# First layer's stored values: from SyncE's transfers at the end of the edge count to ScalarE's queue in attention's fifth unit

## The chip, the cores and the metric

The kernel runs on one core of a Trainium2 chip. The metric is device time of one execution in microseconds (us). Engines are named as in the profile: PE (TensorE, with PEld for its weight loads), DVE (VectorE), ACT (ScalarE), POOL (GpSimd) and SP (SyncE, which here only issues transfers).

## The reference

A graph of 1250 nodes with 512 features and 20000 edges. After a layer norm come two layers of graph attention with 8 heads, each followed by a feed-forward net and batch norms; then a small gated MLP on decoded nibbles.

```python
for l in range(L):                       # 2 layers
    q = ((x @ Wq[l].T + bq[l]) * scaling).reshape(n, H, DH)
    k = (x @ Wk[l].T).reshape(n, H, DH)
    v = (x @ Wv[l].T).reshape(n, H, DH)
    scores = jnp.einsum('ehd,ehd->eh', q[tgt], k[srcidx])
    p = jnp.exp(scores - m[tgt])         # softmax over each target's edges
    agg = segment_sum(w[:, :, None] * v[srcidx], tgt)
    x = _batchnorm(x + agg.reshape(n, D) @ Wo[l].T + bo[l], ...)
    x = _batchnorm(x + relu(x @ W1[l].T + b1[l]) @ W2[l].T + b2[l], ...)
```

## The kernel before

Attention is computed densely: how often an edge joins each pair of nodes is counted into a 1250 by 1250 matrix, whose logarithm (or a very negative number where there is no edge) is added to the scores as a bias. The program is a row of blocks. At the end of a block every engine waits until all engines have come to its end; a transfer need only be issued by then, not landed.

**First block (edge count and first layer's projections).** For each of ten tiles of 125 targets PE counts edges, ACT takes logarithms, DVE combines, and SP stores the tile to `edge_bias` in DRAM (`bias_out`, L536). In the gaps, and after the last tile, PE runs the projections in the order of `JOBS`: q, then v, then k. ACT copies v out of PSUM twice: the first four heads into `v_pair`, where attention will use them, and all of it into `v_stage` (both in `projected`). The keys are split into a high part (`k_stack`, ACT, L344) and a low part (`k_lo`, DVE, L376). The low part of each chunk c of 128 features is copied by SP to the other 64 partitions of `k_stack` (`k_stacked`, L401, two transfers of 64 partitions by 1250 numbers). The block's SP program ends with `stacked` for the first two passes' queries (L461), `k_stacked` for chunks 0 and 1, `values_out`, and `k_stacked` for chunks 2 and 3. `values_out` (L406) stores `v_stage`, 1250 by 512 numbers, to the DRAM tensor `values` in two transfers, of 120 and of 5 partitions (2400 and 100 KB). PE ends the block with 12 idle matmuls (`keep_clock`, L103).

**Attention block of each layer.** A pass n is one pair of heads by one group of two target tiles; 20 passes of 4 units make 80 units u. The program of each engine is written in slots. In slot s, PE computes the three score pieces of unit s (L945) and transposes the probabilities of unit s-3 (L959), and in two of four slots it multiplies a finished pass by the values (L974). DVE adds the bias and finds the peaks (L1041, L1064), copies the middle transposed piece (L1032) and forms the inverse of the mass (L1048, L1050). ACT in slot s copies the first transposed piece of unit s-3 (L1000), takes the exponential of unit s-1 (L1011), and copies the third piece of unit s-3 (L1000). POOL divides (L925) and splits the queries (L449, L451). A pass's output is copied to `attn` by ACT (`out_of`, L1007), first in slot 10. `attn` lies in the same SBUF region as `v_stage`, so the first `out_of` waits until `values` is stored. SP loads the rest of the bias in four parts (`bias_part`, L894: three tiles before `stacked(2)`, four after `stacked(3)`), stacks the queries of pass n (`stacked`, L461), and from the third pair of heads on needs `values` to load `v_pair` (L890). `stacked(3)` waits for all stacked keys, `stacked(4)` for the stored values.

The second layer's projections lie in the block before its attention; there SP issues `values_out` too, long before the block ends.

Of the kernel before, what the change touches and what calls it, by code (L numbers as in the profile page):

```python
# [20 lines left out]
NT = 125  # L21
TILES = N // NT
DC = D // P
# [21 lines left out]
def gnn_ffn(nc, x, src, dst, gnn, ffn, out):  # L45
    ctx = ExitStack()
    with ctx:
        def sem(name):
            return ctx.enter_context(nc.semaphore(name))
# [10 lines left out]
        def place(name, shape, dt, region, offset=0):  # L60
            return nc.alloc_sbuf_tensor_at(name, shape, dt, offset=at[region] + offset)
# [30 lines left out]
        v_d = nc.dram_tensor("values", [N, D], F32, kind="Internal").ap()  # L92
# [3 lines left out]
        def f32(ap):  # L96
            return ap.bitcast(F32)
# [116 lines left out]
        v_stage = place("v_stage", [NT, TILES, D], F32, "RA")  # L214
# [27 lines left out]
        v_stored = sem("v_stored")  # L242
# [12 lines left out]
        def weight(w, c):  # L255
            return w.rearrange("l (c p) i -> p (l c) i", p=P)
# [27 lines left out]
        def split_count(layer, t):  # L284

            return sum(job[0] in SPLIT for job in JOBS[layer][:t])
# [100 lines left out]
        def vectors(sp, layer):  # L387

            for name, col, n in (("bq", BQ, DC), ("bo", BO, DC), ("b2", B2, DC), ("g1", G1, DC), ("beta1", BE1, DC),
                                 ("g2", G2, DC), ("beta2", BE2, DC), ("b1", B1, FC)):  # L390
                with nc.allow_non_contiguous_dma("one column per 128 features"):
                    sp.dma_start(vec[:, col:col + n],
                                 gnn[name].rearrange("l (c p) -> p (l c)", p=P)[:, layer * n:(layer + 1) * n]).then_inc(proj["vec"], 16)

        def k_stacked(sp, layer, c):

            sp.wait_ge(proj["done"], split_count(layer, JOBS[layer].index(("k", c, 2)) + 1))
            for half in range(2):
                own, other = slice(half * DH, half * DH + DH), slice((1 - half) * DH, (1 - half) * DH + DH)
                cols = slice((2 * c + half) * N, (2 * c + half + 1) * N)  # L400
                sp.dma_start(f32(k_stack[other, cols]), f32(k_lo[c % 2][own, :])).then_inc(k_stored[c % 2], 16)  # L401

        def values_out(sp):

            for rows in SPREAD:
                sp.dma_start(v_d.rearrange("(t p) d -> p t d", p=NT)[rows, :, :], v_stage[rows, :, :]).then_inc(v_stored, 16)  # L406

        def first_bias(sp):

            bv = bias_d.rearrange("(t p) s -> p t s", p=NT)  # L410
            for rows in SPREAD:
                sp.dma_start(scores_bias[rows, 0:GROUP, :], bv[rows, 0:GROUP, :]).then_inc(bias_in[0], 16)
            for rows in SPREAD:
                sp.dma_start(scores_bias[rows, GROUP:GROUP + 1, :], bv[rows, GROUP:GROUP + 1, :]).then_inc(bias_in[1], 16)
# [104 lines left out]
        with nc.Block(no_gpsimd_drain=True) as block:  # L519
            @block.sync  # L520
            def _(sp):
                sp.dma_start(e_int[:, 0, :], dst.rearrange("(p e) -> p e", e=2 * NT)).then_inc(e_in, 16)
                sp.dma_start(e_int[:, 1, :], src.rearrange("(p e) -> p e", e=2 * NT)).then_inc(e_in, 16)
                xv = x.rearrange("(t p) d -> p t d", p=NT)
                for k, tiles in enumerate(LOADS_X):
                    for rows in SPREAD:
                        sp.dma_start(xs[rows, tiles, :], xv[rows, tiles, :]).then_inc(x_in[k], 16)
                sp.dma_start(w_nat[0]["wq"][:, :, :], weight(gnn["Wq"], DC)[:, 0:DC, :]).then_inc(proj["wq"], 16)
                sp.dma_start(shift_all[:, :], gnn["ln_b"].rearrange("(a n) -> a n", a=1).to_broadcast([NT, D])).then_inc(shift_in, 16)
                vectors(sp, 0)  # L530
                bv = bias_d.rearrange("(t p) s -> p t s", p=NT)

                def bias_out(j):
                    sp.wait_ge(bias_ready, j + 1)
                    for rows in SPREAD:
                        sp.dma_start(bv[rows, j:j + 1, :], bias_row[rows, j % 2:j % 2 + 1, :]).then_inc(bias_stored[j % 2], 16)  # L536

                def shifted(k):
                    sp.wait_ge(x_shifted, 2 - k)
                    for rows in SPREAD:  # L540
                        sp.dma_start(shifted_d.rearrange("(t p) d -> p t d", p=NT)[rows, PARTS_X[k], :],
                                     xs[rows, PARTS_X[k], :]).then_inc(shifted_stored[k], 16)

                def residual(j0, j1):

                    sp.wait_ge(h_kept, j1)
                    cols = slice(j0 * NT, j1 * NT)
                    for c in range(0, DC, 2):
                        sp.dma_start(res_d[:, c:c + 2, cols], t2[:, c:c + 2, cols]).then_inc(res_stored, 16)

                def turned_out(name):

                    sp.wait_ge(proj["filled"], JOBS[0].index((name, DC - 1)) + 1)

                bias_out(0)
                turned_out("wq")
                sp.dma_start(w_nat[0]["wv"][:, :, :], weight(gnn["Wv"], DC)[:, 0:DC, :]).then_inc(proj["wv"], 16)
                bias_out(1)
                bias_out(2)
                residual(0, 8)  # L560
                bias_out(3)
                residual(8, TILES)
                shifted(1)
                bias_out(4)
                shifted(0)
                turned_out("wv")
                sp.dma_start(w_nat[0]["wk"][:, :, :], weight(gnn["Wk"], DC)[:, 0:DC, :]).then_inc(wk_in, 16)
                for j in range(5, TILES - 1):
                    bias_out(j)
                for s in q_in:  # L570
                    sp.sem_inc(s, 1)
                sp.wait_ge(proj["copied"], len(V_JOBS) + len(Q_JOBS))
                sp.wait_ge(bias_stored[0], 32 * (TILES // 2))
                sp.wait_ge(bias_stored[1], 32 * (TILES // 2 - 1))
                first_bias(sp)
                bias_out(TILES - 1)
                for n in range(2):
                    stacked(sp, n)
                for c in range(2):
                    k_stacked(sp, 0, c)  # L580
                values_out(sp)
                for c in range(2, DC):
                    k_stacked(sp, 0, c)

            @block.gpsimd
# [292 lines left out]
        for layer in range(LAYERS):  # L878
            last_layer = layer == LAYERS - 1
            with nc.Block(no_gpsimd_drain=True) as block:  # L880
# [113 lines left out]
                @block.scalar  # L994
                def _(act):
                    act.sem_inc(att["o_free"], 1)

                    def copy(t, to, of):
                        act.wait_ge(att["t_ready"], t + 1)
                        nc.scalar.activation(to, of, ACT.Copy).then_inc(att["t_free0"], 1)  # L1000

                    def out_of(n):
                        if n == 0:
                            act.wait_ge(v_stored, 32)
                        act.wait_ge(att["o_ready"], n + 1)
                        c, g = divmod(n, GROUPS)
                        nc.scalar.activation(attn[:, c, g * GN:(g + 1) * GN], pb[:, 7, 0:GN], ACT.Copy).then_inc(att["o_free"], 1)  # L1007

                    def exponent(u):
                        act.wait_ge(att["neg_peak"], u + 1)  # L1010
                        nc.scalar.activation(probs[:, u % 4, :], probs[:, u % 4, :], ACT.Exp, bias=neg_peak[:, u % 4:u % 4 + 1],  # L1011
                                             accum_out=mass[:, u % 4:u % 4 + 1]).then_inc(att["exp"], 1)

                    for slot in range(SLOTS + 1):
                        n, piece = divmod(slot - PV_LAG - max(PV_BATCHES) - 1, 4)
                        if n >= 0 and piece == 0:
                            out_of(n)
                        u = slot - T_LAG
                        if 0 <= u < UNITS:
                            bring(0, u, copy, PARTS[:1])  # L1020
                        if 0 <= slot - 1 < UNITS:
                            exponent(slot - 1)
                        if 0 <= u < UNITS:
                            bring(0, u, copy, PARTS[2:])
# [712 lines left out]
```

## Time and profile before

| | |
|---|---|
| Median of 3 runs | 1128.81 us (1127.66 to 1129.23) |
| Profiled execution, its own time | 1131.2 us |
| Span of the profiled execution | 1129.4 us |
| PE busy | 1039.0 us, 92% of the span |
| DVE busy | 776.4 us, 69% |
| ACT busy | 594.2 us, 53% |
| POOL busy | 307.4 us, 27% |
| Transfers of the hardware queue | 83.92 MB, 30.3% of 16 engines' span |

The span runs from the first to the last recorded instruction; the execution's own time is 1.8 us longer. Times inside the trace are microseconds from the span's start. The first attention block begins near 259 us, the second near 711 us.

### The profile page before, as it was taken

To read this page: it belongs to the slowest core of one execution; us is meant where nothing else is said; L and a number is where in the kernel's file an instruction comes from. 1 tells how busy PE (TensorE), PEld (TensorE's weight loads), DVE (VectorE), ACT (ScalarE), POOL (GpSimd) and SP (SyncE) were. 2 spreads that over 40 slices of the span, in tenths; PEclk is the share of its full clock that TensorE was granted. 3 is DMA by queue.
4 is the path that set the end of the run, shared out by engine and by line. 5 is a ranking of instruction groups with operands and counts; after the bars stand their busy time and mean duration, and the time that the engine had idled before them with its cause. 6 is when DMAs were issued, how large, how long until landed. Compare 5 with 4: busy or idle time off the path is not lost. (4 is left out here: it accounts for less than half of the span.)

```text
span 1129.4 us, 18973 instructions
## 1 busy us (share of the span) xinstructions
PE 1039.0 (92%) x6636; PEld 863.6 (76%) x6636; DVE 776.4 (69%) x2429; ACT 594.2 (53%) x1108; POOL 307.4 (27%) x306
## 2 busy tenths in 40 slices
PE   4799899997999999999899999899999999989943
PEld 2577677796888888888799889788888888879832
DVE  6667565756777777777388720677777777738788
ACT  5453223245666666666425532566666666643444
POOL 1000000003444444443032200344444444303204
PEclk9989899998999999999999999999999999999975
DMA  6034301376612112113303445461211211323103
GB/s 143 23 92 140 115 23 44 87 179 150 127 38 60 38 37 60 38 37 110 112 1 112 100 112 122 91 127 37 60 38 37 60 37 38 110 85 63 36 1 92
DMA packets 51073, 85.10 MB, mean 75 GB/s; under 512 B 15519, under 2 KB 33819, under 8 KB 50725
## 3 DMA queue, kind: packets, MB, share of 16 engines
q1 hardware_dynamic: 50980, 83.92, 30.3%
q8 instruction: 52, 0.85, 0.3%
q14 instruction: 41, 0.33, 0.1%
HBM read 36.50 MB, written 21.61 MB: 51 GB/s over the span
## 5 line engine op out<-in xcount | busy, mean ns | idle before, releaser
L925 POOL TENSOR_SCALAR probs<-probs,mass_inv 125x1250 f32<-125x1250 f32 x160 | 211.0, 1319 | 343.8 <-DVE mass_inv L1050 343.8
L1041 DVE CUSTOM_DVE_ANT_0 probs<-banks,scores_bias 125x416 f32<-125x416 f32 (+1 forms) x480 | 267.5, 583 | 50.8 <-PE banks L945 46.4
L945 PE MATMUL banks<-k_stack,q_stack 128*125 128x416 f32 (+1 forms) x960 | 296.0, 394 | 6.6 <-DVEq L1028 6.6
L959 PE MATMUL banks<-ident,probs 125*125 125x125 f32 x1600 | 258.5, 276 | 7.9 <-DVE probs_t L1032 5.9
L959 PEld LDWEIGHTS banks<-ident,probs 125*125 125x125 f32 x1600 | 240.5, 187 | 31.4 <-issue 22.3
L1011 ACT ACTIVATE probs<-probs,neg_peak 125x1250 f32<-125x1250 f32 x160 | 213.4, 1334 | 55.1 <-DVE neg_peak L1064 55.1
L1000 ACT ACTIVATE probs_t<-banks 125x500 f32<-125x500 f32 x320 | 152.6, 477 | 107.8 <-PE banks L959 107.7
L974 PE MATMUL banks<-probs_t,v_pair 125*64 125x250 f32 x1600 | 186.2, 379 | 0.9 <-ACT probs_t L1000 0.9
L945 PEld LDWEIGHTS banks<-k_stack,q_stack 128*125 128x125 f32 x960 | 145.2, 189 | 34.8 <-issue 20.8
L974 PEld LDWEIGHTS banks<-probs_t,v_pair 125*64 125x64 f32 x1600 | 107.5, 136 | 54.3 <-ACT probs_t L1000 1.3
L1032 DVE COPY probs_t<-banks 125x500 f32<-125x500 f32 x160 | 108.2, 676 | 54.6 <-PE banks L959 54.6
L831 PE MATMUL banks<-onehot_src,onehot_dst 125*125 125x512 bf16 x540 | 103.8, 352 | 3.5 <-DVE onehot_src L746 3.4
L831 PEld LDWEIGHTS banks<-onehot_src,onehot_dst 125*125 125x125 bf16 x540 | 69.0, 142 | 37.9 <-issue 11.4
L449 POOL CAST q_split<-q_t 128x250 fp32r<-128x250 f32 x40 | 15.8, 396 | 299.3 <-PE banks L318 208.7
L746 DVE TENSOR_SCALAR onehot_src<-iota,e_col 125x1250 bf16<-125x1250 f16 x180 | 87.2, 542 | 0.0
L1048 DVE TENSOR_SCALAR mass<-mass 125x1 f32<-125x1 f32 x160 | 24.7, 154 | 69.8 <-ACT probs L1011 69.8
L668 ACT ACTIVATE more<-banks 125x1250 f32<-125x1250 f32 x10 | 12.2, 1217 | 97.1 <-PE banks L836 89.1
L743 DVE TENSOR_TENSOR onehot_dst<-iota,e_col 125x375 bf16<-125x375 f16 x60 | 32.9, 548 | 43.3 <-PE banks L831 40.2
L333 PE MATMUL banks<-h_hi,wt_hi 128*128 128x416 f32 (+1 forms) x160 | 57.7, 360 | 3.6 <-ACT h_lo L662 3.1
L333 PE MATMUL banks<-h_hi,wt_lo 128*128 128x416 f32 (+1 forms) x160 | 57.0, 356 | 0.0
L333 PE MATMUL banks<-h_lo,wt_hi 128*128 128x416 f32 (+1 forms) x160 | 57.0, 356 | 0.0
L1097 POOL TENSOR_TENSOR h_lo<-t,h_hi 128x1250 fp32r<-128x1250 f32 x9 | 26.0, 2889 | 100.8 <-ACT h_hi L1275 100.8
(251 smaller groups left out, 1440.3 us busy)
## 6 DMA issues: line engine op xcount, KB each, us to landing
q_stack<-q_split SPq DMA_DIRECT2D x160, 125.0 KB, 2.3
scores_bias<-edge_bias SPq DMA_DIRECT2D x8, 1171.9 KB
edge_bias<-bias_row SPq DMA_DIRECT2D x10, 585.9 KB
k_stack<-k_lo SPq DMA_DIRECT2D x16, 312.5 KB, 4.4
resid<-residual SPq DMA_DIRECT2D x2, 2500.0 KB, 9.9
values<-v_stage SPq DMA_DIRECT2D x2, 2400.0 KB
residual<-t SPq DMA_DIRECT2D x4, 625.0 KB, 3.0
xs<-in_x SPq DMA_DIRECT2D x5, 480.0 KB
```

Source lines behind the costliest of these rows:

```text
L333: mm = nc.tensor.matmul(bank[:, 0:sn], w[:, i, c * P:(c + 1) * P], h[:, i, s0:s0 + sn], **edge)
L743: nc.vector.tensor_tensor(onehot_dst[:, ks.start:ks.stop, 0:NT], own.to_broadcast([NT, STEP, NT]), targets.to_broadcast([NT, STEP, NT]), A ...
L746: op = nc.vector.tensor_scalar(onehot_src[:, k, :], iota[:, :], e_col[:, 1, ds(first + RING * q + k, 1)], None, ALU.is_equal)
L831: last = nc.tensor.matmul(counts[:, s:s + w], onehot_dst[:, k, 0:NT], onehot_src[:, k, s:s + w], start=False, stop=True, skip_group_check= ...
L925: nc.gpsimd.tensor_scalar(probs[:, u % 4, :], probs[:, u % 4, :], mass_inv[:, u % 4:u % 4 + 1], 1.0, ALU.mult, ALU.mult).then_inc(att["pro ...
L945: mm = nc.tensor.matmul(pb[0:NT, t % 5, 0:sn], q_stack[:, n % 2, half, part, tile * NT:(tile + 1) * NT], k_stack[:, head * N + s0:head * N ...
L959: mm = nc.tensor.transpose(pb[0:NT, 5 + t % 2, j * NT:(j + 1) * NT], probs[:, u % 4, (j0 + j) * NT:(j0 + j + 1) * NT], ident[0:NT, 0:NT])
L974: mm = nc.tensor.matmul(pb[half * DH:(half + 1) * DH, 7, 0:GN], v_pair[:, c % 2, j, half * DH:(half + 1) * DH], probs_t[:, n % 2, half, j, ...
L1000: nc.scalar.activation(to, of, ACT.Copy).then_inc(att["t_free0"], 1)
L1011: nc.scalar.activation(probs[:, u % 4, :], probs[:, u % 4, :], ACT.Exp, bias=neg_peak[:, u % 4:u % 4 + 1], accum_out=mass[:, u % 4:u % 4 + ...
L1032: nc.vector.tensor_copy(to, of).then_inc(att["t_free1"], 1)
L1041: nc.vector.tensor_tensor_reduce(out=probs[:, slot % 4, s0:s0 + sn], in0=pb[0:NT, t % 5, 0:sn], in1=scores_bias[:, (n % GROUPS) * GROUP + ...
```

## The change

`values_out` takes the engine that issues. In the first layer it is no longer called in SP's program of the edge-count block, but in ACT's program of the attention block, at the head of slot 4, ahead of the copy of unit 1's first piece. The second layer keeps SP's call.

```diff
-        def values_out(sp):
+        def values_out(engine):
 
             for rows in SPREAD:
-                sp.dma_start(v_d.rearrange("(t p) d -> p t d", p=NT)[rows, :, :], v_stage[rows, :, :]).then_inc(v_stored, 16)
+                engine.dma_start(v_d.rearrange("(t p) d -> p t d", p=NT)[rows, :, :], v_stage[rows, :, :]).then_inc(v_stored, 16)
@@
-                for c in range(2):
-                    k_stacked(sp, 0, c)
-                values_out(sp)
-                for c in range(2, DC):
+                for c in range(DC):
                     k_stacked(sp, 0, c)
@@
                         if n >= 0 and piece == 0:
                             out_of(n)
+                        if slot == 4 and layer == 0:
+                            values_out(act)
                         u = slot - T_LAG
```

SP's instructions at the end of the edge-count block and the start of attention, before. `L401` is a key transfer, `L406` a store of the values, `L894` a load of the bias.

```order
L461 DMA q_stack_114<-q_split_113 64x500 x8
L401 DMA k_stack_106<-k_lo0_98 64x1250 x2
L401 DMA k_stack_106<-k_lo1_99 64x1250 x2
L406 DMA values<-v_stage_108 120x10x512
L406 DMA values<-v_stage_108 5x10x512
L401 DMA k_stack_106<-k_lo0_98 64x1250 x2
L401 DMA k_stack_106<-k_lo1_99 64x1250 x2
L519 UNCONDITIONAL_BRANCH
L881 UNCONDITIONAL_BRANCH
L894 DMA scores_bias_109<-edge_bias 120x1250
```

The same place with the change (the program is three lines shorter there, so L894 has become L891):

```order
L461 DMA q_stack_114<-q_split_113 64x500 x8
L401 DMA k_stack_106<-k_lo0_98 64x1250 x2
L401 DMA k_stack_106<-k_lo1_99 64x1250 x2
L401 DMA k_stack_106<-k_lo0_98 64x1250 x2
L401 DMA k_stack_106<-k_lo1_99 64x1250 x2
L519 UNCONDITIONAL_BRANCH
L878 UNCONDITIONAL_BRANCH
L891 DMA scores_bias_109<-edge_bias 120x1250
```

The two stores are gone from between the keys of chunks 1 and 2; nothing else of SP has moved.

ACT's instructions in slots 1 to 4 of attention, before: exponentials of units 0 and 1, then of slot 3 a copy, the exponential of unit 2 and a copy, then slot 4.

```order
L1011 ACTIVATE probs_110,mass_57<-probs_110,neg_peak_56 125x1250 x2
L1000 ACTIVATE probs_t_111<-banks 125x4x125
L1011 ACTIVATE probs_110,mass_57<-probs_110,neg_peak_56 125x1250
L1000 ACTIVATE probs_t_111<-banks 125x2x125
L1000 ACTIVATE probs_t_111<-banks 125x4x125
L1011 ACTIVATE probs_110,mass_57<-probs_110,neg_peak_56 125x1250
```

The same place with the change (L1011 has become L1008, L1000 has become L997):

```order
L1008 ACTIVATE probs_110,mass_57<-probs_110,neg_peak_56 125x1250 x2
L997 ACTIVATE probs_t_111<-banks 125x4x125
L1008 ACTIVATE probs_110,mass_57<-probs_110,neg_peak_56 125x1250
L997 ACTIVATE probs_t_111<-banks 125x2x125
L406 DMA values<-v_stage_108 120x10x512
L406 DMA values<-v_stage_108 5x10x512
L997 ACTIVATE probs_t_111<-banks 125x4x125
L1008 ACTIVATE probs_110,mass_57<-probs_110,neg_peak_56 125x1250
```

The two stores now stand between the last copy of slot 3 and the first copy of slot 4, and the exponential of unit 3 is two places behind them.

## Rows read from the trace of the kernel before

**Rows 1.** Waits in 252 to 262 us: total, times, longest.

```profile
ACT L1011 <- PEq L519: 6.1, 1, 6.1
PE banks L945 <- DVEq L1028: 6.0, 1, 6.0
```

**Rows 2.** Ends of the edge-count block (L519): durations in ns, first and last start.

```profile
L519 PEldq EVENT_SEMAPHORE  x2: 51/51/51, 253.4 to 259.0; - x2
L519 PEldq DRAIN  x1: 2620/2620/2620, 250.7 to 250.7; - x1
L519 ACTq DRAIN  x1: 1064/1064/1064, 252.1 to 252.1; - x1
L519 SPq DRAIN  x1: 113/113/113, 258.7 to 258.7; - x1
```

**Rows 3.** Timeline 241 to 262 us, PEld left out: start, duration, engine, line, operation.

```profile
241.90 4.04 SPq L406 DMA_DIRECT2D values<-v_stage  x2
...
247.45 10.78 SPq L401 DMA_DIRECT2D k_stack<-k_lo  x4
...
252.05 1.04 ACT L344 ACTIVATE k_stack<-banks 64x416 fp32r<-64x416 f32 x2 [1.24 <-PE banks L333]
253.12 1.19 DVE L376 TENSOR_TENSOR k_lo<-banks,k_stack 64x416 fp32r<-64x416 f32 x2 [1.08 <-ACT k_stack L344]
...
259.38 3.12 PE L945 MATMUL banks<-k_stack,q_stack 128*125 128x418 f32 x8 [6.04 <-DVEq L1028]
260.58 0.59 DVE L1041 CUSTOM_DVE_ANT_0 probs<-banks,scores_bias 125x418 f32<-125x418 f32 x1 [6.27 <-PE banks L945]
```

**Rows 4.** L401 on SP, chunk 3's pair of transfers (254.7 to 258.5): ns min/median/max, starts.

```profile
L401 SPq DMA_DIRECT2D k_stack<-k_lo x2: 461/1922/3382, 254.3 to 254.8; - x2
```

**Rows 5.** L401 on SP in 655 to 657, the second layer's last pair.

```profile
L401 SPq DMA_DIRECT2D k_stack<-k_lo x2: 462/530/597, 655.0 to 655.5; - x2
```

**Rows 6.** L406 on SP in 680 to 690, the second layer's stores of the values.

```profile
L406 SPq DMA_DIRECT2D values<-v_stage x2: 330/820/1309, 682.7 to 683.1; - x2
```

**Rows 7.** Busy us by window: PE, PEld, DVE, ACT, POOL; PE clock, DMA share, GB/s.

```profile
240.00:245.00 5.00, 5.00 (x28) 4.93 (x27) 1.99 (x4) 2.06 (x4) 0.00 (x0) 1.00 0.92 241
255.00:260.00 5.00, 0.62 (x2) 0.63 (x3) 0.00 (x0) 0.84 (x1) 0.00 (x0) 0.57 0.93 225
275.00:280.00 5.00, 3.90 (x26) 3.24 (x25) 4.10 (x16) 4.02 (x8) 1.54 (x3) 1.00 0.09 22
```

**Rows 8.** Windows of 1 us at the block boundary, same columns.

```profile
255.00:256.00 1.00, 0.00 (x0) 0.00 (x0) 0.00 (x0) 0.00 (x0) 0.00 (x0) 0.86 0.87 197
262.00:263.00 1.00, 1.00 (x6) 0.97 (x5) 0.96 (x4) 0.33 (x1) 0.00 (x0) 0.72 0.92 200
```

**Rows 9.** Timeline of ACT, 268 to 274 us: slots 3 and 4.

```profile
268.77 1.34 ACT L1011 ACTIVATE probs<-probs,neg_peak 125x1250 f32<-125x1250 f32 x1 [1.00 <-DVE neg_peak L1064]
...
270.11 0.36 ACT L1000 ACTIVATE probs_t<-banks 125x250 f32<-125x250 f32 x1
270.69 0.59 ACT L1000 ACTIVATE probs_t<-banks 125x500 f32<-125x500 f32 x1 [0.22 <-PE banks L959]
271.82 1.34 ACT L1011 ACTIVATE probs<-probs,neg_peak 125x1250 f32<-125x1250 f32 x1 [0.55 <-DVE neg_peak L1064]
```

**Rows 10.** Timeline of SP, 262 to 320 us.

```profile
271.68 14.58 SPq L461 DMA_DIRECT2D q_stack<-q_split  x8
286.30 1.74 SPq L894 DMA_DIRECT2D scores_bias<-edge_bias  x4
```

**Rows 11.** Timeline, PE at the head of slot 8, and ACT's first `out_of`.

```profile
283.39 0.65 PE L945 MATMUL banks<-k_stack,q_stack 128*125 128x418 f32 x2
...
290.61 0.38 ACT L1007 ACTIVATE attn<-banks 128x250 f32<-128x250 f32 x1 [0.88 <-PE banks L974]
```

**Rows 12.** Timeline of the second layer's attention start, 709 to 714 us.

```profile
711.09 3.08 PE L945 MATMUL banks<-k_stack,q_stack 128*125 128x418 f32 x15 [0.57 <-DVEq L1028]
711.86 0.59 DVE L1041 CUSTOM_DVE_ANT_0 probs<-banks,scores_bias 125x418 f32<-125x418 f32 x1 [39.05 <-PE banks L945]
```

## The prediction

> **What bounds the kernel now.** I read the list of waits first, cut to the few microseconds in which the edge-count block gives way to attention. PE stands idle there for 6.0 us and ACT for 6.1 [rows 1], in a kernel whose PE is otherwise busy nearly all the time, and by the list no other PE wait is as long in this stretch. The question is who lets the block end so late. The instructions of the block's end answer it [rows 2]: PE's program reached its drain at 250.7 and was through with it 2.62 us later, at 253.3; ACT's drain began at 252.1 and lasted to 253.2; SP's drain began only at 258.7. All go on at 259.0. So SP is last, by more than 4 us.
>
> What held SP is the pair of transfers for the last key chunk. DVE's last piece of `k_lo` ends at 253.12 + 1.19 = 254.31 [rows 3], and SP issues the first transfer at 254.3. That issue takes 461 ns. The second starts at 254.8 and takes 3382 ns, to 258.2 [rows 4]. The same pair in the second layer, with the transfer engines less loaded, takes 462 and 597 ns, 1.06 us in all from 655.0 [rows 5]. An issue instruction is meant to be short; this one was held for about 2.8 us. The windows say by what: the transfer engines are 92 to 93% busy at 240 to 245 and at 255 to 260, and by 275 to 280 at 9% [rows 7]. The values, 2.5 MB, were issued at 241.9, just ahead of these keys on the same queue, and their two issues took 4.04 us [rows 3] where the second layer's took 0.33 + 1.31 = 1.64 [rows 6].
>
> **The change, part by part.** *The two stores leave SP.* Their 4.04 us of SP time cost nothing themselves: they end at 245.94, and SP's next issue is at 247.45 [rows 3], when chunk 2's low part is ready, so SP waits for DVE in between with or without them. What counts is the queue behind them. Without 2.5 MB of backlog, chunk 3's second issue should take 597 ns in place of 3382 [rows 4, 5]: a gain of 3.382 - 0.597 = 2.785 us. SP is then through at 255.4 instead of 258.2. It is still the last engine at the barrier, because PE and ACT are through at 253.3 and DVE at 254.3 plus its own end; the full 2.8 us is therefore on the path. Everything from 259 us on moves 2.8 us to the left. Below, ACT times are still those of the trace before; subtract 2.8 for the new ones.
>
> *PE's clock.* PE's last matmul ends at 259.38 - 6.04 = 253.34. The granted clock is 1.00 up to there and falls to the lower of its levels, 1.2 GHz, at about 255.7: the mean 0.86 of the window 255 to 256 is 0.72 us at 1.00 and 0.28 us at 0.50. It rises again at about 262.6 [rows 8]. That costs a little: DVE's first piece comes 260.58 - 259.38 = 1.20 us after PE's start [rows 3], while in the second layer, where PE hardly paused (0.57 us), it comes 0.77 us after [rows 12]. With the change PE is idle for 6.04 - 2.79 = 3.25 us, to 256.6, which is still past 255.7. So I count no gain from the clock, with 0.43 us for the first piece, and at most 0.7 us with the following pieces, as the end of the range.
>
> *The two stores come to ACT, in slot 4.* Attention starts up in a loop through DVE and ACT: the exponential waits for DVE's peak, DVE's next two pieces wait in its program behind the mass of that exponential. Exponentials start at 268.77 and 271.82, 3.05 us apart [rows 9]. This loop has no spare time, so a delayed exponential would be lost in full. What matters is how much of the issue time lies in ACT's own gaps. In slot 4 ACT waits 0.22 us before its first copy and 0.55 us before the exponential [rows 9]. Those are 0.77 us against an issue of 1.64 [rows 6].
>
> But an issue is done by ACT's sequencer, not its datapath, and the sequencer runs ahead. Rows 2 and 3 show it: the drain instruction at the end of ACT's first block begins at 252.1, although the two copies ahead of it began at 252.05 and ran to 253.09. In slot 3 the exponential of unit 2 starts at 268.77, and the piece for the copy behind it has long been transposed. I expect the sequencer to hand over both and begin the first store near 268.8, while the datapath computes the exponential and the copy up to 270.47. The stores are then through at 268.8 + 1.64 = 270.4, before the 270.69 at which the next copy starts anyway. Cost: 0. If that cover is gone, because the issue starts only once the copy has ended, it ends at 270.47 + 1.64 = 272.11, the copy of 0.59 takes until 272.70, and the exponential is 272.70 - 271.82 = 0.88 us late. At SP's loaded price of 4.04 us the two starts give 1.6 us (268.8 + 4.04 + 0.59 - 271.82) and 3.3 us. The price is nearer to the second layer's than to this layer's, since on ACT's queue nothing is ahead of the stores, so I take 0 and keep 3.3 as the other end.
>
> *The transfers themselves* are not fewer. They now run from about 269 to 283 (the first layer's windows move some 0.22 MB per us, so 2.5 MB take 11 to 12 us), when the engines are at 9% for part of the time [rows 7]. The stacked queries of pass 2 are issued at 271.68 [rows 10] and PE needs them at 283.39 [rows 11]: 11 us for what is a small transfer. The next bias loads are issued at 286.30, after the stores are through. `out_of` at 290.61 needs the stored values [rows 11]: 7 us of slack. `stacked(4)` is later still. I cost all of these at nothing; the cover is these gaps.
>
> *Sum:* -2.8 + 0 + 0 = -2.8 us. Against the profiled execution that is 1131.2 - 2.8 = 1128.4, span 1126.6; the median of the runs is 2.4 us lower than this execution, and from it the forecast is 1128.81 - 2.8 = 1126.0.
>
> **Rivals.** *ACT's issue is exposed.* The sequencer doesn't begin until the datapath is empty. For it: a queue of instructions may behave otherwise around a transfer than around a drain, and the trace before has no transfer issued by ACT. Against it: rows 2. Time: -2.8 + 0.9 = -1.9, so 1126.9.
>
> *ACT's issue is held as SP's was.* When it comes, the keys and three bias tiles, 2.5 MB in all, are just landing (issued 254 to 258 new time, 11 to 12 us at 0.22 MB per us, so to about 266 to 268; the stores come near 266). Then 4.04 us apply: -2.8 + 1.6 to -2.8 + 3.3, that is 1127.6 to 1129.3. Perfetto Trace Analysis in the Trainium skill, on the HWDGE instruction, gives a way to this: the generator of descriptors is shared and locked by one sequencer at a time, and the profiled time of an issue holds that wait. The trace agrees so far that a short store behind a long one takes 1309 ns (or the reverse) [rows 6], and that by the order of issue SP should not be issuing anything near 266. I leave this at a small chance.
>
> *Slower: ACT is held until its own transfer has nearly drained.* SP's held issues show that an issue can wait for the engines. If 2.5 MB on ACT's queue hold its sequencer for the 11.6 us that they take, the exponential of unit 3 is late by 268.8 + 11.6 + 0.6 - 271.8 = 9.2 us, in a loop without slack, and the time is 1128.8 - 2.8 + 9.2 = 1135.2. It decides from an issue of 5.2 us on; against it stands that the second layer's stores went out in 1.64 us.
>
> *The gain is not there.* Something other than the values held the last key issue: the two for chunk 2, or the barrier is bound elsewhere, or bytes in flight count and not their place. DMA: Bandwidth & Descriptors in the Trainium skill, on issuing engines, speaks for that: all queues share the same 16 engines and interleave, and another issuing engine saves only the sequencer's issue time. Taken alone it gives the 4.04 us of SP's issue time back, which lie in front of a wait, so 0. Time: 1128.8. Against it, the stores are not only on another queue but some 25 us later.
>
> **How the numbers follow.** Forecast (hidden issue, barrier 2.8 us earlier): 0.57, of which 0.12 with up to 0.7 us more from the clock (1125.3). Exposed: 0.16. Held: 0.11. No gain: 0.10. Held to the end: 0.06. The bound for telling a change from none is 0.2%, 2.3 us. The forecast lies 0.5 us beyond it, and the runs of before spread over 1.6 us, so a part of it would read as the same: faster 0.53, same 0.40, slower 0.07. The range goes from 1125.1 (clock gain and a little scatter) to 1128.4, which takes in the exposed case and half of the held one and leaves out no gain and the slow one.
>
> **What would show it.** In the profile after: chunk 3's second issue near 0.6 us; SP's drain near 255.9 instead of 258.7; PE's idle time at the boundary 3.2 us instead of 6.0; two L406 on ACT's queue near 266, 1.6 us together, starting while the exponential of unit 2 runs; exponentials of units 2 and 3 still 3.05 us apart. An exponential of unit 3 that starts more than 3.1 us after that of unit 2 shows the exposed or held case and its price; an unchanged 3.4 us issue at the barrier shows the gain was never the values'. I would be wrong altogether if PE waited for stacked queries at slot 8 or ACT for the stored values at slot 10.

## The result: slower by 0.24%

| | before | with the change |
|---|---|---|
| Median of 20 runs each | 1128.18 us | 1130.73 us |
| Lowest to highest | 1124.87 to 1132.96 | 1128.92 to 1133.69 |
| Ratio | | 1.0024, 95% interval 1.0014 to 1.0034 |
| Profiled execution, span | 1131.2, 1129.4 us | 1131.37, 1129.6 us |

The forecast was 2.8 us less; it became 2.5 us more. The gain at the block boundary came as forecast. The loss is some 26 us behind it.

**The boundary, answering to [rows 1, 2, 4].** PE's wait in 250 to 262 us (total, times, longest), with the change:

```profile
PE banks L942 <- DVEq L1027: 3.0, 1, 3.0
```

and SP's issues for the last key chunk (durations in ns, then first and last start):

```profile
L401 SPq DMA_DIRECT2D k_stack<-k_lo x2: 461/530/599, 252.4 to 252.9; - x2
```

PE idles 3.0 us instead of 6.0, and the second issue takes 599 ns instead of 3382. That is 3.0 us of gain where 2.8 was forecast.

**ACT's stores, answering to [rows 9].** ACT's timeline, 263 to 268 us:

```profile
263.14 1.34 ACT L1008 ACTIVATE probs<-probs,neg_peak 125x1250 f32<-125x1250 f32 x1 [1.00 <-DVE neg_peak L1063]
263.15 2.60 ACTq L406 DMA_DIRECT2D values<-v_stage  x2
...
264.48 0.36 ACT L997 ACTIVATE probs_t<-banks 125x250 f32<-125x250 f32 x1
265.80 0.59 ACT L997 ACTIVATE probs_t<-banks 125x500 f32<-125x500 f32 x1 [0.96 <-PE banks L956]
266.28 1.33 ACT L1008 ACTIVATE probs<-probs,neg_peak 125x1250 f32<-125x1250 f32 x1
```

The issue begins 0.01 us after the exponential of unit 2 and runs beside it, as expected. It takes 2.6 us, not 1.64, and ends at 265.75. The view names PE for the 0.96 us before the copy of 0.59 us, but the copy starts 0.05 us after the issue's end and 2.66 us after the exponential of unit 2, where it was 1.92 before [rows 9]: the issue held it by 0.74 us. (In e6 below, where the issue takes 1.34 us, it is 1.92 again.) The gap of 0.55 us that ACT has before its next exponential takes up most of that. The exponential of unit 3 follows after 3.14 us instead of 3.05, so the price that is left on ACT is 0.09 us.

**Slot 8, answering to [rows 10, 11].** The waits in 262 to 300 us that name a transfer, then PE's timeline at the head of slot 8, then SP's four issues for pass 2 with their time to landing:

```profile
POOL q_split L449 <- DMA q_stack<-q_split: 5.4, 1, 5.4
...
PE banks L942 <- DMA q_stack<-q_split: 3.0, 1, 3.0
```

```profile
280.95 1.06 PE L942 MATMUL banks<-k_stack,q_stack 128*125 128x418 f32 x2 [3.02 <-DMA q_stack<-q_split]
```

```profile
L461 SPq DMA_DIRECT2D q_stack<-q_split x4: 467/2318/2996, 266.0 to 271.3; - x4
...
DMA to landing us min/median/max: 8.6/9.4/10.6
```

This is the new wait. Before, PE went into slot 8 with no wait on a transfer. Now the stacked queries of pass 2, issued from 266.0 on, are held at issue (up to 3.0 us each, where 0.6 is usual) and land 8.6 to 10.6 us after their issue began (2.2 to 2.4 in e1 below, where the stores come after them), and PE stands for 3.02 us. The pair of matmuls behind the wait takes 1.06 us; at full clock such a pair takes 0.65 [rows 11]. The windows show why (columns as in [rows 7]):

```profile
278.00:280.00 2.00, 0.00 (x0) 0.00 (x0) 0.40 (x3) 0.00 (x0) 0.00 (x0) 1.00 0.37 107
280.00:282.00 2.00, 1.05 (x3) 1.01 (x4) 0.00 (x0) 0.00 (x0) 0.95 (x2) 0.55 0.04 16
...
284.00:286.00 2.00, 2.00 (x9) 1.92 (x9) 1.55 (x6) 1.18 (x3) 0.55 (x1) 0.50 1.03 209
286.00:288.00 2.00, 2.00 (x13) 1.99 (x12) 1.08 (x6) 0.94 (x2) 0.76 (x1) 0.74 0.84 213
```

After the idle stretch the granted clock is at its lower level, 1.2 GHz, from about 280.2 (0.55 is the mean of 280 to 282) to 287.0. PE works through all but the first 0.75 us of that. From the start of slot 8 to ACT's first `out_of` it is 7.22 us before (283.39 to 290.61 [rows 11]) and 9.93 with the change (280.95 to 290.88): 2.71 us more.

**A finer measure than the time.** Runs of one kernel spread over 5 to 8 us, and the profiles tell where much of it arises: PE's last matmul of the edge-count block ends at 253.34 before, at 251.39 with the change, and between 248.4 and 253.7 in the experiments, though PE's program up to there is the same but for the idle matmuls of two of them. From the last `attn` copy of the first layer to that of the second, by contrast, it is 451.0 to 451.1 us in all fourteen profiles. So I compare the stretch from PE's end in the edge-count block to the start of the last `attn` copy of the first layer; it holds all that the change can touch. It is 296.35 us before and 298.50 with the change: +2.15, which agrees with the runs' +2.5. Its sum: -3.03 (idle at the boundary, 6.04 to 3.01), -0.65 (start of attention at full clock: first exponential 2.64 us after PE's first scores, 3.29 before), +0.09 (ACT), +3.02 (the wait). That makes -0.57, so 2.72 us remain for the lower clock behind the wait, which agrees with the 2.71 read above.

### The profile page after: what moved, and what is told of

Read it like the earlier page. It is cut to its first block and busy times, and to the rows that moved or that the text cites. A ratio compares the mean times of both kernels' runs of the same rounds, so it can differ in the third digit from the quotient of the medians.

```text
span 1129.6 us, 18973 instructions
## 1 busy us (share of the span) xinstructions
PE 1037.7 (92%) x6636; PEld 861.0 (76%) x6636; DVE 775.7 (69%) x2429; ACT 593.8 (53%) x1108; POOL 307.5 (27%) x306
## 5 line engine op out<-in xcount | busy, mean ns | idle before, releaser
L1008 ACT ACTIVATE probs<-probs,neg_peak 125x1250 f32<-125x1250 f32 x160 | 213.4, 1334 | 53.4 <-DVE neg_peak L1063 53.4
L997 ACT ACTIVATE probs_t<-banks 125x500 f32<-125x500 f32 x320 | 152.6, 478 | 114.1 <-PE banks L956 114.1
```

## The experiments

All are compared with runs of the kernel before on the same chip, whose medians lie between 1128.16 and 1128.49 us. e2 and e9 have 5 runs each and e5 has 6, the others 10 to 12; so medians of two experiments that lie within 2 us are not told apart by these times. "Stretch" is the measure above, of one profiled execution each.

| run | median, us | ratio (95% interval) | stretch, us |
|---|---|---|---|
| before | 1128.2 | | 296.35 |
| the change | 1130.73 | 1.0024 (1.0014 to 1.0034) | 298.50 |
| e1_slot6 | 1131.18 | 1.0033 (1.0021 to 1.0045) | 300.65 |
| e2_sp_before_q2 | 1124.08 | 0.9967 (0.9955 to 0.998) | 293.72 |
| e3_sp_after_q2 | 1129.11 | 1.0011 (0.9999 to 1.0022) | 296.63 |
| e4_clock | 1128.94 | 1.0013 (1.0002 to 1.0025) | 296.49 |
| e5_sp_late | 1131.36 | 1.0034 (1.0021 to 1.0048) | 300.51 |
| e6_act_half | 1125.19 | 0.9976 (0.9963 to 0.9988) | 293.29 |
| e7_sp_half | 1125.92 | 0.9983 (0.9973 to 0.9993) | 293.38 |
| e8_before_half | 1126.03 | 0.9981 (0.9969 to 0.9992) | 293.43 |
| e9_half_clock | 1123.73 | 0.9952 (0.9935 to 0.997) | 290.91 |
| e10_slot6_half | 1125.89 | 0.9982 (0.997 to 0.9995) | 293.29 |
| e11_slot0 | 1127.47 | 0.9986 (0.9974 to 0.9998) | 294.55 |
| e12_sp_clock | 1125.98 | 0.997 (0.9958 to 0.9981) | 292.08 |

In e9 and e12, 16 added idle matmuls (1.75 us: 3.23 for 28 less 1.48 for 12) lie ahead of PE's end; with them back, the stretches are 292.66 and 293.83.

### e1: ScalarE's stores two slots later

```diff
-                        if slot == 4 and layer == 0:
+                        if slot == 6 and layer == 0:
```

> ScalarE issues the stores in slot 6 instead of slot 4. Theory (transfers collide): the 2.5 MB of stores were on the engines just when pass 2's stacked queries were issued (266 us), these landed only at about 281, and PE stood idle 3.0 us at the head of slot 8 and then ran 6 us at the lower clock. Two slots later the stacked queries are through first: their four issues take 0.5 to 0.6 us each, no PE wait at slot 8, clock 1.00 from 276 to 290, PE idle at the block boundary still about 3.1 us. Time 5 to 6 us under the changed kernel and 2.5 to 3.5 under the kernel before, about 1125. Rival (a store issued by ScalarE costs in itself, whatever the slot): the loss stays, 1130 to 1131. Second rival (moved, not removed): the wait turns up at slot 10, where attn waits for the stored values, 1127 to 1130.

The wait at slot 8 is gone, as the first theory has it, but the time is the worst but one. Two new waits took its place; from the waits in 285 to 302 us:

```profile
DVE probs L1040 <- DMA scores_bias<-edge_bias: 4.4, 1, 4.4
...
ACT attn L1004 <- DMA values<-v_stage: 3.7, 1, 3.7
```

The second rival was right, and only half of it: ACT waits 3.7 us at slot 10 for the stored values, and DVE 4.4 us at slot 12 for the bias. SP's program explains the latter. Its issues for pass 3's queries are held behind the stores (up to 2.8 us each), and the bias load comes behind them in SP's program, so it goes out only at 284.6, 35.9 us after PE's end, where it went out 33.0 us after it before [rows 10].

### e2 and e3: the same stores on SyncE, ahead of or behind pass 2's queries

```diff
+                    if layer == 0:
+                        values_out(sp)        # e2
                     stacked(sp, 2)
+                    if layer == 0:
+                        values_out(sp)        # e3
```

In both, ACT's call in slot 4 is taken out.

> SyncE issues the stores in the attention block, after the three bias tiles and ahead of pass 2's stacked queries: one queue, in order. Theory by bytes (no matter which queue): from 254 us on the engines must carry 0.6 MB of keys, 1.9 of bias, 2.6 of values and 0.5 of queries, 5.6 MB at about 0.22 MB per us, so the queries, last in order, land near 279.5; PE waits 1 to 2.5 us at slot 8, with or without the lower clock after it: 1126 to 1129. Rival (it is the second queue: the queries' small pieces take turns with the other queue's large ones and lose): in one queue there are no turns, the queries land by 278, no wait, 1125.

> SyncE issues the stores in the attention block right behind pass 2's stacked queries. Theory (order on the engines decides): queries of pass 2 land within 5 us, no PE wait at slot 8; pass 3's queries queue behind the stores and have until slot 12; attn's wait at slot 10 is met with some us to spare. About 1125, like e1. Rival (SyncE's issue at the boundary was never worth 2.8 us at the end): within 1 us of the kernel before, 1128.

e2 beat both kernels: PE's wait at slot 8 is 0.3 us, less than my count of bytes gave. Taken alone that speaks for the rival, two queues that take turns; e5 is the test of it. e3 went as e1 did: its queries for pass 2 took 2.3 us to land, and then the waits were 1.4 us for the values and 3.2 us for the bias at slot 12. My expectation of 1125 for e3 was wrong; what the boundary gave was spent on these two waits. So there is no free place for 2.5 MB behind pass 2's queries either: each place moves the wait to the next user of the transfers.

### e4: the clock behind the wait

```diff
+                        if slot == 8 and layer == 0:
+                            pe.wait_ge(att["s_free"], 3 * slot + 1)
+                            keep_clock(3 * slot % 5, 26)
```

> The changed kernel with 26 idle matmuls (128x256 bf16, 0.12 us each) on PE at the head of slot 8, which fill the wait for the queries. Theory (the loss is 3.0 us of waiting and 2.7 us of lower clock after it: from slot 8's start to the first copy of attn 7.22 us before and 9.93 after): the wait stays but the clock is 1.00 behind it, 2 to 3 us under the changed kernel, about 1128.2. Rival (only the wait counts, PE makes up for the clock elsewhere): no gain, 1130.7.

POOL's wait for the same queries is 5.4 us as in the change, and PE's first pair of scores in slot 8, behind the idle matmuls, runs at full clock:

```profile
275.46 3.01 PE L103 MATMUL banks<-ident 128*128 128x256 bf16 x26
278.60 0.65 PE L942 MATMUL banks<-k_stack,q_stack 128*125 128x418 f32 x2
```

The stretch is 2.01 us shorter, although this execution had the lower clock at the boundary, which cost it 0.64 us (first exponential at 3.28 instead of 2.64). Together 2.65 us: the 2.72 us left over in the sum above. From the start of slot 8 to the first `out_of` it is 7.22 us, as before (278.60 to 285.82). The medians, 1128.94 and 1130.73, go the same way by 1.8 us, less than the 2 to 3 expected, and their intervals overlap, so it is the trace that decides. The first theory holds: the loss behind the boundary is 3.0 us of waiting and about 2.7 of clock.

### e5: the same moment, but SyncE's own queue

```diff
+                    if layer == 0:
+                        sp.wait_ge(att["s_free"], 5 + 9)
+                        values_out(sp)
                     stacked(sp, 2)
```

> The stores go out at the same moment as in the changed kernel (SyncE waits for unit 2's scores, near 263), but on SyncE's own queue, ahead of pass 2's stacked queries. Measure: from PE's end in the edge-count block to the last copy of attn in the first layer, 296.35 us before, 298.50 in the changed kernel. Theory A (bytes on the engines, whatever the queue): the queries land as late as in the changed kernel, 29 us after PE's end, PE waits about 3 us, the measure is 298 to 299, time 1130 to 1131. Theory B (a second queue makes the queries take turns with the stores and lose): in one queue they land near 27.5 us after PE's end, PE waits under 1 us, the measure is 293.5 to 294.5, time 1125 to 1126.

```profile
L461 SPq DMA_DIRECT2D q_stack<-q_split x4: 467/2340/2578, 265.7 to 271.0; - x4
...
PE banks L945 <- DMA q_stack<-q_split: 5.3, 1, 5.3
```

Theory B is refuted: in one queue the queries land 10.9 to 11.8 us after their issue, later than from two queues, and PE waits 5.3 us. It is not ScalarE's queue that does the harm. Theory A was nearer, and too mild by 2 us.

### e6, e7, e8: half of the bytes

Only columns 256 to 511 of `values` are ever read back, since the first two pairs of heads take theirs from `v_pair`. Each of the three stores only these in the first layer: e6 from ScalarE in slot 4, e7 in e2's place, e8 in the old place of the kernel before.

```diff
-                            values_out(act)
+                            values_out(act, slice(4 * DH, D))
```

> The changed kernel, but the first layer stores only the second half of the columns (256 to 511), the only ones that are read back: 1.28 MB instead of 2.56, still from ScalarE in slot 4. Theory (the collision of the stores with pass 2's queries costs the 3 us wait and the clock after it): half of the bytes are through some 6 us earlier, the queries land before slot 8, no PE wait; the measure from PE's end to the last attn copy falls from 298.50 to 293 to 294, time about 1125. Rival (the cost comes from the form of it, two queues at once or an issue by ScalarE): the wait only halves, 296 to 297, 1128 to 1129.

> SyncE's stores ahead of pass 2's queries (as in the run that gave 1124.1), but the second half of the columns alone. Theory: the last 0.3 us of wait at slot 8 and POOL's 2.6 us go; the measure is 293.0 to 293.7 (it was 293.72), the time within 1 us of 1124.1. If the time falls by 2 us or more, the stores still cost something there that the trace did not show as a wait.

> The kernel before, with the stores in their old place on SyncE, and only the second half of the columns. Theory (the last key transfer's issue was held for 2.8 us by the backlog of the stores): 1.28 MB less is 5.8 us less of backlog, the last issue takes 0.6 us, PE's idle time at the block boundary falls from 6.0 to about 3.0, the measure to 293 to 293.7, time about 1125. Rival (something else holds the issue, such as the keys of chunk 2): the issue stays above 2.5 us and the time at 1128.

e6 is the change itself with its suspected cost halved, and it gives the gain that the prediction promised the change: no engine waits for a transfer at slot 8, the stretch is 3.06 us under that of before, the time 3.0. e8 is the other half of the argument, with nothing moved at all. Its last key issues and the wait at the boundary:

```profile
L401 SPq DMA_DIRECT2D k_stack<-k_lo x2: 461/530/599, 250.0 to 250.5; - x2
```

```profile
PE banks L945 <- DVEq L1028: 3.2, 1, 3.2
```

The issue that took 3382 ns takes 599 once 1.28 MB less lie ahead of it. So the backlog of stores held the barrier. e7 came out as expected in the stretch; its median is 1.8 us above e2's, outside the 1 us expected. The stretch (0.3 shorter) does not support that, and the intervals of the two ratios overlap.

### e9 and e10: what else is at the boundary, and slot 6 again

e9 is e6 with more idle matmuls at PE's end in the edge-count block; e10 is e6 with its store in slot 6.

```diff
-                keep_clock(bank_of(0, len(JOBS[0])), 12)
+                keep_clock(bank_of(0, len(JOBS[0])), 28)
```

> ScalarE's half store in slot 4, and 28 instead of 12 idle matmuls at PE's end in the edge-count block, 2.0 us more, which fill most of the 3.0 us that PE idles at the boundary. Theory (with a pause of 3 us the clock falls in some executions and the first exponential comes 3.28 us instead of 2.64 us after PE's first scores): the clock stays at 1.00, first exponential at 2.64, and the block boundary comes no later, since SyncE is last there by more than 2 us: 0.3 to 0.7 us under the half store alone, 1124.5 to 1125. Rival (PE becomes the last at the barrier): the boundary moves out by up to 1 us and the gain is gone.

> ScalarE's store in slot 6, as in the run that lost 4.3 us in the measure (waits of 3.7 us for the stored values at slot 10 and 4.4 us for the bias at slot 12), but half of the columns. Theory (those waits are the bytes of the stores, met later): both waits vanish, the measure is 293.2 to 293.8, time about 1125. Rival (slot 6 is too late for SyncE's next issues in any case): a wait for the bias of over 1 us stays at slot 12, measure above 295.

e9 has the lowest median and the shortest stretch: 1123.73 us in 5 runs, ratio 0.9952 (0.9935 to 0.997), faster than both kernels; against e6 the stretch with the matmuls put back is 0.63 us shorter. PE's pause is 1.27 us, the first exponential comes at 2.64, and SP, whose drain starts at 254.1 when PE's ends at 253.7, is still the last. In the pauses of 3.0 to 3.2 us of the other runs the clock stayed up in two profiles (the change and e3) and fell in nine; in the two pauses of 1.27 us (e9, e12) it stayed up. e10's two waits are gone: with half of the bytes slot 6 is as good as slot 4, so e1's waits were bytes too.

### e11 and e12: full stores, issued early

e11 is the change with `slot == 0`; e12 is e2 with 28 idle matmuls.

> ScalarE issues the full stores in slot 0, nine us earlier than the changed kernel, beside SyncE's loads of three bias tiles. Theory (when the stores come decides, not which queue): as with SyncE's stores right behind the bias loads, which left 0.3 us of wait at slot 8, the queries of pass 2 land in time, the wait is under 1 us, the measure from PE's end to the last attn copy is 293.3 to 294.5, time 1124 to 1126. Rival (ScalarE's queue beside SyncE's delays what SyncE has issued): bias tile 3 or the last keys come late and DVE waits for the bias at slot 4 by 1 us or more; measure above 295.

> SyncE's full stores ahead of pass 2's queries (as in the run that gave 1124.1), with 28 instead of 12 idle matmuls at the block's end. Theory: the wait at slot 8 stays under 1 us, and the first exponential comes 2.64 us after PE's first scores instead of 3.28: the measure, with the 1.75 us of added matmuls put back, is near 293.1, time 1123.5 to 1124.5. This is also a second look at how fast the stores move there: the first showed 356 to 389 GB/s in six windows of 1 us, in every other run they show 180 to 300. If that was chance of one execution, the wait at slot 8 is 1 to 5 us in this one and the time 1125 to 1129.

e11 has no wait for a transfer at slot 8, nor at slot 4, but its stretch is 294.55, just above the upper end, and its time of 1127.47 us is 1.5 above what I expected, for a reason of its own. ACT's timeline:

```profile
254.83 3.33 ACTq L406 DMA_DIRECT2D values<-v_stage  x2
258.20 1.28 ACT L1008 ACT_TABLE_LOAD   x1 [6.50 <-issue]
259.49 1.34 ACT L1008 ACTIVATE probs<-probs,neg_peak 125x1250 f32<-125x1250 f32 x1
```

Here the issue has nothing to hide under: the table load stands behind it in the program, and the first exponential is 1.25 us late (4.53 us after PE's first scores, not 3.28). This is the exposed issue that the prediction had as a rival, in the place where it is real. e12 confirms e2: a wait of 1.1 us at slot 8, and the fast stores again, 373 to 395 GB/s in the five windows from 265 to 270. Both the wait and the time, 1125.98 us, are above what I expected (under 1 us, 1123.5 to 1124.5), and the stretch with the matmuls put back, 293.83, is 0.7 above it; the wait is the one new thing that its trace shows there.

## Why the prediction was wrong

- **What bounds the boundary: right.** SP was last, held by the backlog of the stores. e8 shows it without moving anything.
- **The two stores leave SP, -2.8: right.** PE's idle time fell by 3.03 us, where the difference of the two issues gave 2.79.
- **The clock at the boundary, 0 with 0.7 at the end of the range: right in kind.** It gave 0.65 us in the change's profile, and nothing in most of the others. The argument for 0 was that a pause of 3.25 us reaches past 2.4 us, after which the clock had fallen before. A pause of 3.01 us did not lower it in this execution, so that argument forecasts most executions and not each.
- **ACT's issue, cost 0: right by 0.09 us, but not by the cover that was counted.** It began beside the exponential as forecast. It took 2.6 us instead of the 1.64 taken from the second layer, so it ended behind the moment at which the next copy could start and held it by 0.74 us; only ACT's gap before the exponential hid that. By the prediction's own sign (more than 3.1 us between the exponentials) this is the exposed or held case, at a price of 0.09 us; it began beside the exponential, so it is the held one.
- **The two rules behind rivals.** Perfetto Trace Analysis in the Trainium skill, on the HWDGE instruction, has one sequencer at a time lock the shared generator of descriptors. Nothing in this trace needs that: SP issues nothing between 256.5 and 266.05, and ACT's issue runs from 263.15 to 265.75. (Rows 6, which the prediction set beside that rule, are two issues of one sequencer and say nothing of a wait between two.) DMA: Bandwidth & Descriptors in the Trainium skill, on issuing engines, has the transfers of all issuers run on the same 16 engines and interleave. With that the trace agrees: with ScalarE's stores in flight SyncE's query transfers took 8.6 to 10.6 us to land instead of 2.2 to 2.4, and that was the loss. That another issuing engine saves only issue time is not tested by the change, since it also sends the stores 23 us later, counted from PE's end.
- **"The transfers themselves ... I cost all of these at nothing": this step failed.** It set 11 us of slack for pass 2's queries against their own landing, as for "a small transfer", while the sentence before said that the stores would keep the engines busy until 283, in the old count of time, when the queries were needed at 283.39. The two numbers were never put together. The engines are not left for the queries while 2.5 MB are ahead of or beside them. From the prediction's own figures the queries' 0.5 MB would have followed the stores to 285 (2.3 us at 0.22 MB per us), 2 us late. (269 and 11 to 12 us give 280 to 281 and not 283; about 283 comes out if the keys and the bias tiles ahead of the stores are counted too, as under the rival of the held issue. Even from 281 the queries would be in at 283.3, with 0.1 us to spare and not 11.) Measured were 3.0 us, and 2.7 us of clock on top.
- **The rate behind it was right, the end of the backlog was not.** 2.5 MB were priced at 11 to 12 us by the mean rate of mixed traffic. With the change, the engines stay 0.86 busy or more from 257 to 277, and the windows of 1 us from 253 to 277 sum to 5.2 MB, 0.22 MB per us. But from 277 to 281 only 0.4 MB follow, and it is 280.95 before the last queries are in.
- **The same collision stood in the trace of before, in the second layer.** There the full stores are issued at 682.7, and the next four query transfers 8 us behind them:

```profile
L461 SPq DMA_DIRECT2D q_stack<-q_split x4: 468/2699/2797, 690.6 to 696.6; - x4
...
DMA to landing us min/median/max: 5.2/6.8/7.3
```

They are held up to 2.8 us each and take up to 7.3 us to land, where the first layer's took 2.2 to 3.1. No PE wait shows it, since they are not needed before 711. The prediction took the price of the issue from these stores and did not look at what was issued behind them.

- **The idle engines at 275 to 280 [rows 7] were read as room.** They were idle because the stores had been sent at 241.9, more than 30 us before. The room existed only before the first user of the transfers came, and e1 and e3 show that behind that user there is the next.
- **The rivals.** None of them was this one. The closing paragraph named the sign, PE waiting for stacked queries at slot 8, without a price or a chance; it deserved both, as the rival on the slower side, in place of the one with ScalarE held for 11.6 us.

## What to carry to other kernels

When a large transfer is moved to where the queue looks free, list the transfers that are issued after it and need to land soon, and set the whole backlog, not their own landing time, against the moment they are needed. Look in the trace of before for a place where the same transfer already runs, and at what is issued behind it. A short wait of a busy PE costs more than its length when the clock falls in it: here 3.0 us became 5.7. And before moving bytes, see whether they must be moved at all: half of these were never read, and leaving them out gave the gain in each of the four places tried.

## What the runs showed of the hardware that was not expected

The rate of the same stores depends on when they are issued. In slot 4 or near it they share the engines at 173 to 302 GB/s in windows of 1 us from 264 to 276, whichever queue issues them (the change, e5). Issued by SyncE directly behind the bias loads the engines moved 334 to 389 GB/s in e2 (six windows from 264), 373 to 395 in e12 (five from 265) and, with half of the bytes, 337 to 368 in e7 (four from 265), and beside the loads, from ScalarE in slot 0, the engines moved 277 to 361 GB/s from 260 to 273 us. In all of these windows the engines show as 0.87 busy or more. e2 and e5 send the same bytes in the same order through one queue, 7 us apart, with the engines 0.8 busy or more from 253 to 272 in both. Up to 264 both have moved 2.3 MB, and until all have landed 5.4 MB; e2 needs until 277 for that and e5 until 283. PE waits 0.3 us in one and 5.3 us in the other, and this difference in rate is what separates them.

It is the high rate that is the exception. The second layer's stores go out with no other transfer of the program beside them, and this is the window of before:

```profile
685.00:690.00 5.00, 5.00 (x29) 4.94 (x28) 0.00 (x0) 1.22 (x2) 0.55 (x2) 1.00 0.94 195
```

e1's stores, with pass 2's queries landed and pass 3's not yet issued, show the same 195 GB/s from 269 to 275. So the small transfers of the queries are not what slows the stores in slot 4. What lets them go faster right behind or beside the bias loads, no run here isolates, and it stays open.

The queries' landing has a long tail: in the last 3 us before PE goes on, the engines are only 0.09 to 0.46 busy (windows of 1 us, 278 to 281, with the change). So the mean share of busy engines says too little about when a transfer lands. Whether a few engines are late or all of them work with gaps, the views don't show.
